# The product (I + W0)(I + W1) by seven products of quarters

## The reference

```python
x = x + (x @ W0.T + b0) + scale[id0] * (x @ A0[id0].T) @ B0[id0].T     # id0 in 1..7
x = x + (x @ W1.T + b1) + (x @ A1[id1].T) @ B1[id1].T                  # id1 in 6..15
x = x + x @ W2[id2].T                                                  # one of 8 matrices per batch
x = x + einsum('bct,bcd->bdt', x, W3[id3])                             # 64 x 64 per batch
```

## Time and profile of the kernel before

| | |
|---|---|
| median of three runs | 580.36 us |
| the profiled execution: its own time | 580.31 us |
| its span (first to last instruction) | 578.5 us |
| TensorE busy | 568.8 us, 98% of the span, 2706 matmuls recorded |
| VectorE / ScalarE / GpSimd busy | 280.9 / 246.4 / 58.9 us |
| granted TensorE clock | 1.000 |
| DMA | 60.92 MB, 105 GB/s on average |

### The profile page before, as it was taken

The page is one execution under the profiler, slowest core; times in us unless marked ns, Lnnn a source line. Parts: engine busy times, 40 slices in busy tenths (PEclk is TensorE's granted clock), DMA queues, the critical chain, the costliest instruction groups (busy, mean ns, idle before and its releaser), DMA issues.

```text
span 578.5 us, 10382 instructions
## 1 busy us (share of the span) xinstructions
PE 568.8 (98%) x2706; PEld 475.3 (82%) x2707; DVE 280.9 (49%) x519; ACT 246.4 (43%) x307; POOL 58.9 (10%) x87
## 2 busy tenths in 40 slices
PE   8999999999999999999999999999999989999997
PEld 6888888888888788888888888888888878888885
DVE  5986211122666356743445684333568349634210
ACT  5633210214643628444252755335365538353201
POOL 3350000200000030000002100000121030000000
PEclk9999999999999999999999999999999999999999
DMA  8855835101207223453221436321233623230103
GB/s 287 261 180 86 87 101 195 45 18 56 91 15 275 76 51 135 125 210 93 57 64 48 132 119 223 85 65 58 53 127 87 256 54 116 57 95 17 40 1 73
DMA packets 66158, 60.92 MB, mean 105 GB/s; under 512 B 42067, under 2 KB 50259, under 8 KB 66133
## 3 DMA queue, kind: packets, MB, share of 16 engines
q1 hardware_dynamic: 66132, 60.63, 35.6%
HBM read 49.33 MB, written 11.27 MB: 105 GB/s over the span
## 4 chain that ended last, share of the span: by engine, by line
PE 97%; DMA 1%; DVE 0%; issue 0%; ACT 0%; SPq 0%; POOL 0%; POOLq 0%
PE y_ps L1251 30%; PE y_ps L1286 27%; PE y_ps L1201 11%; PE t_ps L1201 6%; PE t_ps L1278 5%; PE low_ps L1241 3%; PE y_ps L1314 3%; PE y_ps L1182 3%; PE t_ps L1182 1%; PE y_ps L1267 1%; PE low_ps L1182 1%; PE y_ps L1266 1%; PE y_ps L1178 1%; PE y_ps L1300 1%; PE t_ps L1192 1%; DMA arena<-w 1%
## 5 line engine op out<-in xcount | busy, mean ns | idle before, releaser
L1251 PE MATMUL y_ps<-wm,ops 128*128 128x512 f32 x768 | 179.6, 391 | 0.0
L1251 PEld LDWEIGHTS y_ps<-wm,ops 128*128 128x128 f32 x768 | 141.9, 188 | 28.9
L1286 PE MATMUL y_ps<-ring,ops 128*128 128x512 f32 x696 | 164.5, 392 | 0.5 <-issue 0.5
L1286 PEld LDWEIGHTS y_ps<-ring,ops 128*128 128x128 f32 x696 | 129.6, 188 | 27.6 <-issue 0.9
L591 ACT CAST ops<-arena 128x512 fp32r<-128x512 f32 x32 | 19.8, 621 | 96.4 <-PE y_ps L1251 96.4
L1201 PE MATMUL y_ps<-ring,wm 128*128 128x512 f32 x240 | 55.3, 390 | 0.0
L997 DVE TENSOR_TENSOR ops<-t_ps,ops 128x512 fp32r<-128x512 f32 x32 | 22.1, 690 | 64.5 <-ACT ops L644 54.7
L1201 PEld LDWEIGHTS y_ps<-ring,wm 128*128 128x128 f32 x240 | 44.9, 188 | 9.3
L644 ACT CAST ops<-t_ps 128x512 fp32r<-128x512 f32 x32 | 18.7, 589 | 79.0 <-PE t_ps L1278 78.7
L985 DVE TENSOR_TENSOR ring<-arena,ring 128x1024 fp32r<-128x1024 f32 x40 | 48.4, 1246 | 5.7 <-ACT ring L622 4.9
L492 POOL TENSOR_TENSOR w_stage<-w_stage,ident 128x128 f32<-128x128 f32 x16 | 11.3, 704 | 371.3 <-DMA w_stage<-w 371.3
(11 more groups left out here) (149 smaller groups left out, 560.1 us busy)
## 6 DMA issues: line engine op xcount, KB each, us to landing
arena<-wt SPq DMA_DIRECT2D x48, 512.0 KB, 4.4
arena<-xt SPq DMA_DIRECT2D x32, 256.0 KB, 2.8
out<-arena SPq DMA_DIRECT2D x30, 256.0 KB, 3.1
a_stage<-a_tab SPq DMA_DIRECT2D x64, 64.0 KB, 1.9
arena<-b_tab SPq DMA_DIRECT2D x64, 64.0 KB, 2.0
arena<-w SPq DMA_DIRECT2D x7, 576.0 KB, 6.2
arena<-a_cols SPq DMA_DIRECT2D x8, 256.0 KB, 4.4
a_tab<-bias SPq DMA_DIRECT2D x4, 256.0 KB, 8.4
```

Of the source, the lines that this page charges most:

```text
L1251: op = nc.tensor.matmul(main_ps(j)[:, cols], xs[:, k, part_x, :], wm[:, k, part_w, cols], start=k == 0 and part_x == part_w, stop=False)
L1286: op = nc.tensor.matmul(y[:, cols], xs2[:, k, part_x, :], ring[:, k, part_w, cols], start=k == 0 and part_x == part_w, stop=k == KT - 1 an ...
```

## The change

M is computed by the seven products of Winograd's form of Strassen's scheme. With W0 + I in quarters A11, A12, A21, A22 and W1 + I in quarters B11 to B22:

S1 = A21 + A22, S2 = S1 - A11, S3 = A11 - A21, S4 = A12 - S2; T1 = B12 - B11, T2 = B22 - T1, T3 = B22 - B12, T4 = B21 - T2. Then M11 = A11 B11 + A12 B21; with U = A11 B11 + S3 T3 and V = U + S2 T2: M21 = V + A22 T4, M22 = V + S1 T1, and M12 = A11 B11 + S2 T2 + S1 T1 + S4 B22. Each product has four block rows of 4 k tiles x 3 parts = 12 matmuls, 336 in all.

GpSimd makes the sums S, VectorE the sums T, from fresh copies of W0 and W1, which SyncE loads again in pairs of tiles into three buffers (`PAIR_OF`): pairs 0 to 3 of W0 for S3 and S2, 4 to 7 of W1 for T3, T2 and T4, 8 and 9 of W1 for T1, 10 to 13 of W0 for S4 and S1. The sums are split as other operands and take the places of quarters that are no longer needed (`s3, t3, t4, t1, s4, s1`), so a cast waits until the product before has been finished. Partial sums of M lie in SBUF (`AT_M1`, `AT_M2`, `AT_M3`) and are added on VectorE. Three further edits: the first loads come in another order (A1 first, W0's tile 0 in two halves of its own, the columns of B0 behind them), with finer waits in `a1_products`; in the second pair `finish_low(1)`, the third matrix load `layer3_of(1)` and `between_loras(1)` move forward; and the last of the four final stores is issued by ScalarE.

```diff
+PAIR_OF = (0, 1, 2, 0, 1, 2, 0, 1, 2, 0, 2, 0, 2, 0)
+FIRST_S, FIRST_T, SECOND_T, SECOND_S = 0, 4, 8, 10
...
+AT_PAIR = 0, 2 * FEATS, WAITING * FEATS
...
+        a11, a12 = wm[:, HK:, :, FIRST], wm[:, HK:, :, SECOND]
+        a21, a22 = wm[:, :HK, :, FIRST], wm[:, :HK, :, SECOND]
+        b11, b12 = ring[:, :HK, :, FIRST], ring[:, :HK, :, SECOND]
+        b21, b22 = ring[:, HK:, :, FIRST], ring[:, HK:, :, SECOND]
+        s2, t2 = (ops[:, n * HK * FEATS:(n + 1) * HK * FEATS].rearrange("p (k s n) -> p k s n", s=2, n=BANK)
+                  for n in range(2))
+        s3, t3, t4, t1, s4, s1 = a21, b12, b11, b21, a12, b12
...
+        PS_FIRST = [y2_ps[:, BANKS[0]], y2_ps[:, BANKS[1]], t_ps[:, BANKS[1]], t_ps[:, BANKS[0]]]
+        PS_TURN = [t_ps[:, BANKS[1]], t_ps[:, BANKS[0]], t_ps[:, BANKS[1]], t_ps[:, BANKS[0]]]
+        PS_LONG = [y_ps[:, BANKS[0]], y_ps[:, BANKS[1]], y2_ps[:, BANKS[0]], y2_ps[:, BANKS[1]]]
...
-            sp.dma_start(slot(0)[:, half:FEATS + N0_COLS], w0[0][:, half:]).then_inc(w0_part_in, 16)
             sp.dma_start(slot(0)[:, FEATS + N0_COLS:], a1_cols[0]).then_inc(a1_in[0], 16)
+            sp.dma_start(slot(0)[:, half:FEATS], w0[0][:, half:FEATS]).then_inc(w0_part_in, 16)
             sp.dma_start(slot(0)[:, 0:half], w0[0][:, 0:half]).then_inc(slot_in[0], 16)
+            sp.dma_start(slot(0)[:, FEATS:FEATS + N0_COLS], w0[0][:, FEATS:]).then_inc(b0_part_in, 16)
...
+            sp.wait_ge(acc_w_step, KT - 2)
+            load_w0(0, 0, BANK)
+            store_a1(range(2))
+            sp.wait_ge(acc_w_step, KT - 1)
+            load_w0(1, 1, BANK)
+            store_a1(range(2, 4))
+            sp.wait_ge(acc_w_step, KT)
+            load_w0(2, 2, BANK)
+            store_a1(range(4, 5))
+            sp.wait_ge(s2_lo, 1)
+            load_w0(3, 3, BANK)
+            store_a1(range(5, 7))
+            sp.wait_ge(s2_lo, 2)
+            load_w1(4, (0, HK))
+            store_a1(range(7, KT))
             sp.wait_ge(evictions, KT + 1)
             sp.dma_start(g_tab.rearrange("e r n -> (e r) n"), evicted(KT)).then_inc(g_stored, 16)
+            sp.wait_ge(s2_lo, 3)
+            load_w1(5, (1, HK + 1))
             sp.wait_ge(b0_ready, 1)
             sp.dma_start(b0_tab.rearrange("e r n -> (e r) n"), b0_rows).then_inc(b0_stored, 16)
...
+            sp.wait_ge(s2_lo, 4)
+            load_w1(6, (2, HK + 2))
+            sp.wait_ge(t4_lo, 1)
+            load_w1(7, (3, HK + 3))
+            sp.wait_ge(t4_lo, 2)
+            load_w1(8, (0, 1))
+            sp.wait_ge(t4_lo, 3)
+            load_w1(9, (2, 3))
...
+            sp.wait_ge(t1_lo, 2)
+            load_w0(10, 0)
+            sp.wait_ge(t1_lo, 4)
+            load_w0(11, 1)
...
+            sp.wait_ge(s1_lo, 1)
+            load_w0(12, 2)
+            sp.wait_ge(s1_lo, 2)
+            load_w0(13, 3)
             for n in range(EVICTIONS):
                 sp.wait_ge(a1_stored[n], 16 * KT // EVICTIONS)
+            sp.wait_ge(d_stored, 16)
...
+            sp.wait_ge(s1_lo, 3)
             load_b(which)
...
+            sp.wait_ge(m12_lo, HK)
+            first_matrix(range(HK, KT))
             b_rows(1, which)
             which = x_and_a(2)
+            layer3_of(1)
             first_chunks(1)
             b_rows(2, which)
-            layer3_of(1)
...
-                for b in range(2):
+                for b in range(2 - n):
                     sp.dma_start(out[batches[b]][:, cols], out_rows[b * ROWS:(b + 1) * ROWS, cols]).then_inc(stored, 16)
...
+                pool.wait_ge(pair_landed[PAIR_OF[n]], pair_in(n))
+                fold_block(qa21[:, k * P:(k + 1) * P]).then_inc(s_folded, 1)
+                pool.wait_ge(s_folded, k + 1)
+                nc.gpsimd.tensor_tensor(qa22, qa21, qa22, ALU.add).then_inc(s1_sum, 1)
+                nc.gpsimd.tensor_tensor(qa21, qa11, qa21, ALU.subtract).then_inc(s3_sum, 1)
+                pool.wait_ge(s1_sum, k + 1)
+                nc.gpsimd.tensor_tensor(qa11, qa22, qa11, ALU.subtract).then_inc(s2_sum, 1)
...
+                nc.gpsimd.tensor_tensor(qa22, qa21, qa22, ALU.add).then_inc(s1_sum, 1)
+                pool.wait_ge(s1_sum, HK + (k + 1))
+                nc.gpsimd.tensor_tensor(qa11, qa22, qa11, ALU.subtract).then_inc(s2_sum, 1)
+                pool.wait_ge(s2_sum, HK + (k + 1))
+                nc.gpsimd.tensor_tensor(qa12, qa12, qa11, ALU.subtract).then_inc(s4_sum, 1)
...
+                pool.wait_ge(pair_landed[PAIR_OF[n]], pair_in(n))
+                for quarter in (qb11, qb22):
+                    fold_block(quarter[:, k * P:(k + 1) * P]).then_inc(t_folded, 1)
...
+            for k in range(3):
+                first_s(k)
+            fold_t(0)
+            first_s(3)
+            for k in range(1, HK):
+                fold_t(k)
+            fold_t1(SECOND_T)
+            fold_t1(SECOND_T + 1)
             fold_w3(0)
+            for k in range(HK):
+                second_s(k)
...
+            for n in range(5):
+                evict(n)
+            first_s_hi(0)
+            evict(5)
+            evict(6)
+            first_s_hi(1)
+            evict(7)
+            evict(KT)
+            acc_w_hi()
+            first_s_hi(2)
+            keep_m1(0)
+            first_t_hi(0)
+            keep_m1(1)
+            first_s_hi(3)
+            keep_m1(2)
+            take_b0()
+            first_t_hi(1)
+            keep_m1(3)
+            t4_hi_part(0)
+            t4_hi_part(1)
+            m11_hi_part(0)
+            first_t_hi(2)
+            t4_hi_part(2)
+            m11_hi_part(1)
+            first_t_hi(3)
+            t4_hi_part(3)
+            m11_hi_part(2)
+            m11_hi_part(3)
+            for k in range(HK):
+                t1_hi_part(k)
             take_bias()
...
-            take_m(4)
+            for k in range(1, HK):
+                second_s_hi(k)
+            m21_hi_part(0)
+            m21_hi_part(1)
...
+                dve.wait_ge(t_folded, 2 * (k + 1))
+                nc.vector.tensor_tensor(qb11, qb12, qb11, ALU.subtract).then_inc(t1_sum, 1)
+                nc.vector.tensor_tensor(qb12, qb22, qb12, ALU.subtract).then_inc(t3_sum, 1)
+                dve.wait_ge(t1_sum, k + 1)
+                nc.vector.tensor_tensor(qb22, qb22, qb11, ALU.subtract).then_inc(t2_sum, 1)
+                dve.wait_ge(t2_sum, k + 1)
+                nc.vector.tensor_tensor(qb21, qb21, qb22, ALU.subtract).then_inc(t4_sum, 1)
...
+            first_s_lo(0)
+            first_s_lo(1)
+            acc_w_lo()
             order_the_batches()
-            take_m(0)
+            first_s_lo(2)
+            t_sums(0)
+            first_t_lo(0)
             rank_the_matrices()
-            take_m(1)
+            first_s_lo(3)
+            t_sums(1)
+            first_t_lo(1)
             plan_layer2()
-            for i in range(2, 5):
-                take_m(i)
+            t4_lo_part(0)
+            t4_lo_part(1)
+            m11_lo_part(0)
+            t_sums(2)
+            first_t_lo(2)
+            t4_lo_part(2)
+            m11_lo_part(1)
+            t_sums(3)
+            first_t_lo(3)
+            t4_lo_part(3)
+            m11_lo_part(2)
+            for k in range(2):
+                t1_sum_again(k)
+            m11_lo_part(3)
+            for k in range(2, HK):
+                t1_sum_again(k)
+            for k in range(HK):
+                t1_lo_part(k)
+            add_s3_t3(0)
+            acc_a_lo()
+            add_s3_t3(1)
+            add_s3_t3(2)
+            add_s3_t3(3)
+            second_s_lo(0)
+            add_s2_t2(0)
+            second_s_lo(1)
+            add_s2_t2(1)
+            add_s2_t2(2)
+            second_s_lo(2)
+            add_s2_t2(3)
+            sum_m21(0)
+            second_s_lo(3)
+            sum_m21(1)
+            m21_lo_part(0)
+            m21_lo_part(1)
+            a_lo(0)
+            sum_m21(2)
+            b_lo_parts(0)
+            sum_m21(3)
+            m21_lo_part(2)
+            m21_lo_part(3)
+            couple(0)
+            for i in range(HK):
+                sum_m22(i)
+                m22_lo_part(i)
             for h in range(2):
                 x_lo(0, h)
...
+            convert(0, (0,))
+            for i in range(HK - 1):
+                sum_m12(i)
+                m12_lo_part(i)
+                convert(0, (i + 1,))
+            sum_m12(HK - 1)
...
+                pe.wait_ge(evictions, (5, 6, 6, KT + 1)[i])
+                quarter_product(PS_FIRST[i], a11, b11, i, goes_on=True)
...
+                if i < 2:
+                    pe.wait_ge(m11_lo, i + 3)
                 else:
-                    pe.wait_ge(m_lo, i - 2)
-                by_w1(PASS2[i % 3], lambda part, k: wm[:, i, part, k * P:(k + 1) * P], last=i == KT - 1)
+                    pe.wait_ge(m2_ready, i - 1)
+                quarter_product(PS_TURN[i], s3, t3, i, s3_lo, t3_lo)
...
+                pe.wait_ge(m3_ready, i + 1)
+                quarter_product(PS_LONG[i], s1, t1, i, s1_lo, t1_lo, adds=True, goes_on=True)
```

(58 more changed lines are left out.)

385 lines of the change are left out of this document (284 added, 101 removed).

## The result

| | before | after |
|---|---|---|
| median of the runs, us | 580.3 (580.2 to 580.6) | 605.9 (604.1 to 606.2) |
| ratio | | 1.043 (95% interval 1.041 to 1.045) |
| profiled execution, span, us | 580.31, 578.5 | 604.06, 602.3 |
| mean granted clock | 1.00 | 0.976 |
| matmuls of 512 columns for (I + W0)(I + W1) | 384 | 336 |

The account below looks back on a forecast made before the run. TensorE was taken as the bound, 97% of the chain. Savings gave 580.3 - 10.9 - 1.1 - 1.0 - 0.5 = 566.8 us; stalls of 38.1 made 604.9, forecast 605 (595 to 609, chance 0.5), ends 584 and 613.

Parts of the forecast that it names:

- 48 matmuls: Products of M: 384 matmuls become 336, at 0.2267 us each, 10.9 us off the path.
- head, w3 gap, tail: Small edits: earlier lo products at the head 1.1 us, gap before second transposes 1.0, last store on ScalarE 0.5.
- (a): Before `same_products`: pair loads and A1' stores add up on SyncE's DMA queue, so eviction 7 ends late; stall 2.1 us.
- (b): Before the place products: pair 2, store 4 and the W splits delay `order_the_batches` to 77.0; stall 3.4 us.
- (c): Before the rank products: `rank_the_matrices` queues on VectorE behind pair 4's sums and differences, until 88.8; stall 6.1 us.
- (d): At S3 T3: pair 7 lands at 105.6, its differences end at 113.4; stall 12.5 us, plus 1.3 for `add_s3_t3(0)`.
- (e): At A22 T4: GpSimd's second S sums last to 148.2, M21's sums queue behind their splits; stalls 2.2 and 3.3 us.
- (f): Before the first main part: M12's rounds take 3.35 us against TensorE's 2.72, `m12_sum` comes at 183.0; stall 7.2 us.
- GpSimd gets in first: Rival: GpSimd enters after each VectorE instruction; stalls rank 11.3, s3 8.5, A22 T4 10.3, 611 us; with dearer sums chance 0.18.
- faster: Rival: loads slip past the A1' stores, pair 7 comes some 20 us earlier, 567 to 579 us; chance 0.08.
- Cheap sums: Rival: GpSimd's 512-column sum takes 0.6 us, without blocking VectorE, and loads run at 400 GB/s; 582 to 595, chance 0.2.
- signs of being wrong: Pair 4 landing before 76, the 512-column sum under 0.8 us, or TensorE idle under 20 us between 60 and 185.

Follow-up runs that it names:

- run 1: The kernel before, still with eight products, with only the three small edits (first loads, second pair's order, last store on ScalarE): 577.0 us.
- run 5: The changed kernel with 24 matmuls of unused result put into TensorE's wait before the first main part: 603.0 us.
- run 7: The changed kernel with GpSimd's first twelve sums over 16 of their 512 columns: 603.1 us.
- run 6: The changed kernel with the four rounds of M12 in a row, ahead of the conversions of W2: 599.7 us.
- run 2: A1' stored in rows of 2 KB: 580.6 us in the kernel before; the same edit in the changed kernel 592.8 us.
- run 4: The changed kernel with `rank_the_matrices` moved ahead of pair 4's sums T on VectorE: 604.5 us.
- run 9: The changed kernel with 2 KB rows of A1', M12's rounds first and two rounds of reordering, of pair 7 only T3 ahead of S3 T3: 588.4 us.
- run 10: run 9 with three orders mended, among them `add_s3_t3` ahead of the splits of T1 and T2: 581.8 us.
- the last kernel: run 10 with VectorE making eight of GpSimd's twelve second S sums, and VectorE's queue reordered again: 580.0 us.

## Why the prediction was right, and where not

The forecast was 605.0, the profiled execution of after is 604.1, the median 605.9. The ledger by steps:

| step | predicted | measured |
|---|---|---|
| 48 matmuls | -10.9 | 336 left, 0.23 each |
| head, w3 gap, tail | -2.6 | -3.2 (run 1) |
| (a) `same_products` | 2.1 | 1.3 |
| (b) place | 3.4 | 3.2 |
| (c) rank | 6.1 | 9.0 |
| (d) S3 T3 with M1's adds | 13.8 | 3.4 |
| (e) A22 T4 | 5.5 | 2.2 |
| (f) first main part | 7.2 | 7.3 |
| slow clock behind waits | not in it | 9.7 |

The measured column gives 602.3. Of the 1.8 up to 604.1, 0.7 is a gap of TensorE at 240.6, and 0.4 a head that was shorter in run 1 (the product for B0' ended at 65.8 there and at 66.3 in after); the rest was not traced. As said at run 5, each wait can be off by 1 to 2 us from execution to execution.

The stalls were 11.7 us too high in all and the clock was missing with 9.7, so a good part of the hit looks like luck: in the ledger two errors of opposite sign cancel. It is less so than the two sums suggest, because the chain was walked on the engines that set it. `order_the_batches` was to be done at 77.0 and was at 76.9; `m11_lo_part(2)` was to end at 113.4 and ended at 111.7; the sum of M12 was to let TensorE go at 183.0 and did at 180.9. What TensorE does in between, waiting at full clock or working slowly, doesn't move such a point. The 4.4 us of slow clock behind the place and rank products only made TensorE reach S3 T3 later, at 108.4 and not 101.4, and took that much out of the stall there. In the sum only the slow clock behind the last wait is paid in full, 1.8: 604.9 - 2.1 + 1.8 = 604.6. That 604.1 came out and not this is small change both ways: the gap of 0.47 that the edits removed unforeseen, and the new one of 0.7 at 240.6, are in it. What the prediction had wrong is the price of idleness: it put the clock at nothing because it had no row for it, and 9.7 us of slow matmuls stood there, 1.8 of them on the path.

*The prices* held: GpSimd's sum of 512 columns was taken at 1.3 and measures 1.29 to 1.30 alone. VectorE's sums follow at 0.60 where GpSimd is idle, and the first two stores held SyncE 5.51 where 5.9 had been put. The estimate of 1.1 to 1.3 that the prediction made from the 4497 ns of the Trainium skill (GPSIMD Engine Reference, 3.1 Elementwise) for 2048 float32 agrees with the 1.29 to 1.30 at its upper end.

*(c) was mis-sized* by 2.9. I let VectorE's unbroken row keep GpSimd out; in fact they took turns, three of VectorE's four sums at 1.64 to 1.75. That is the rival "GpSimd gets in first" at this place alone (it said 11.3, measured 9.0; its 8.5 and 10.3 further on measured 3.4 and 2.2), and run 7 shows its cause. VectorE was done with the rank at 93.4 and not 88.8, 4.6 later: 1.0 of it is pair 4, whose fold began at 84.2 and not 83.2, and 3.7 the row of sums and differences. TensorE itself reached the place 1.7 late, at 84.5 and not 82.8, by the slow clock behind the place products, which leaves 2.9.

*(d) was mis-sized most*, 3.4 for 13.8. TensorE came 7.0 later, as said. The point it waited for came 1.7 early: with the turns `first_s(3)` ended at 90.5 and not 92.5, and SyncE issued the store of B0' at 93.0 and not 94.7. And the 1.8 for `keep_m1` and `add_s3_t3(0)` never stood on TensorE's path.

*(e) was mis-sized* by 3.3, the second of its two waits. The second S sums ended at 144.7 and not 148.2, so `sum_m21(1)` ended at 147.3, and TensorE, at the slow clock behind the first wait, came to the last block row no sooner.

*(f)* held in mechanism and size. The chain of after shows the rounds (start us, us, what), and ahead of them one of GpSimd's sums:

```profile
121.96 1.30 POOL arena L652
...
174.47 1.05 ACT ring L874
175.54 1.23 DVE ring L1369
177.92 1.05 ACT ring L874
179.00 1.23 DVE ring L1369
180.88 7.40 PE y_ps L1727 x24
```

One round is 3.45, taken at 3.35. Run 6 confirms that what stood between the rounds, the conversions of W2 and x's split, was the price.

*The rival "faster"*, that loads slip past the stores, fell: run 2 shows that the loads did stand behind the stores' short packets. *"Cheap sums"* was wrong on the sum's price (1.3, and not 0.6). Of the prediction's signs of being wrong none came: pair 4's fold began at 84.2, and TensorE's idle time up to 185 us was 26.4.

## What to carry to other kernels

Before an algorithm with fewer matmuls is written, count the sums, splits and loads that it puts between two products, and walk them queue by queue to the points where TensorE needs them; a matmul saved is worth 0.23 us only while none of these points comes late. The loss is set by the last point of such a chain, so mending the largest wait alone (run 4) moves it and gains some 1 us, and short-row stores that cost nothing on one schedule can cost 13 us on the next. Where one engine's queue serves several consumers, put first what TensorE needs next, and look at what then stands behind.

## What the hardware showed that I had not expected

- **The granted clock falls when TensorE waits, and the work behind pays.** Behind waits of 2.2 to 9.0 us in after 24 matmuls took 7.4 to 8.2 us and not 5.60, for part of that time at a granted clock of 0.50 (1.2 GHz), even where the clock had still been 1.00 at the end of the wait; 24 matmuls that fill most of the wait keep it at 1.00 (run 5). The length of the wait alone doesn't decide it: 2.8 us in run 9 were followed by 7.39, and 2.8 us at the same place in run 10 by full clock; 2.2 us in A22 T4 cost 1.8 in after, and 2.4 us at the same place in run 6 left the clock at 1.00. What else decides stays open.
- **VectorE and GpSimd take turns** on two-input sums: VectorE's 512 columns show 0.67 to 0.70 alone, one every 0.60, and 1.64 to 1.75 beside GpSimd's 1.3. It isn't the same everywhere: in run 9 two short folds of GpSimd beside VectorE's row took 3.15 us, where one alone takes 0.46. It also hits VectorE's smallest steps: in run 9 a step of the batch order on 32x33 elements took 1.21 us beside GpSimd's sums; the same step in after, with GpSimd idle, took 0.17. First run 9, then after:

```profile
67.58 1.21 DVE L1125 TENSOR_SCALAR odd<-odd 32x33 int32<-32x33 int32 x1
...
75.39 0.17 DVE L1120 TENSOR_SCALAR odd<-odd 32x33 int32<-32x33 int32 x1
```

- **The reordered seven products scatter more**: 577.4 to 582.9 in 12 runs of the last kernel, beside 579.6 to 581.0 in 17 runs of the kernel before. Its profiled execution (578.95) paid 1.8 us of slow clock behind the wait of 3.7. That the others scatter because they pay more or less of it, or because their waits differ, is argued, not shown.
